# Row maximum of attention scores: one matmul over high and low parts of 128 rows, or two of 64 rows on the two halves of the array

## The reference

```python
qkv = X @ W_qkv + b_qkv                      # (4, 1024, 16 heads x 3 x 64)
Q, K, V = split(qkv)
scores = einsum('bhqd,bhkd->bhqk', Q, K) / sqrt(64)
attn = softmax(scores, axis=-1)
out = einsum('bhqk,bhkv->bhqv', attn, V) @ W_fc + b_fc
```

## Time and profile before

| | |
|---|---|
| median of 3 runs | 1964.52 us (1964.1 to 1965.58) |
| span of the profiled execution | 1962.0 us |
| TensorE busy (matmul) | 1813.4 us, 92% |
| VectorE busy | 1567.3 us, 80% |
| GpSimd busy | 1166.7 us, 59% |
| ScalarE busy | 1081.5 us, 55% |
| mean granted TensorE clock | 0.977 |

### The profile page before, as it was taken

The page is one execution under the profiler, slowest core; times in us unless marked ns, Lnnn a source line. Parts: engine busy times, 40 slices in busy tenths (PEclk is TensorE's granted clock), DMA queues, the critical chain, the costliest instruction groups (busy, mean ns, idle before and its releaser), DMA issues. The chain is left out here.

```text
span 1962.0 us, 29122 instructions
## 1 busy us (share of the span) xinstructions
PE 1813.4 (92%) x7819; PEld 985.8 (50%) x7819; DVE 1567.3 (80%) x2879; ACT 1081.5 (55%) x2008; POOL 1166.7 (59%) x521
## 2 busy tenths in 40 slices
PE   4899999999999999999999999999999999956996
PEld 3444444445544445544444444445544444425886
DVE  5788888888788888888787878887788888677788
ACT  4455555555555555555555555555555555424874
POOL 4465666666666666666666666666666666722124
PEclk8899999999999999999999999999999999967999
DMA  2111111111111111111111111111111110100010
GB/s 88 45 37 33 38 35 35 33 37 37 37 37 37 27 37 28 36 37 37 37 37 32 37 32 34 35 37 37 37 37 37 27 37 28 50 22 22 23 38 27
DMA packets 51521, 70.64 MB, mean 36 GB/s; under 512 B 6269, under 2 KB 29338, under 8 KB 51482
## 3 DMA queue, kind: packets, MB, share of 16 engines
q1 hardware_dynamic: 51328, 70.15, 12.9%
q10 hardware_dynamic: 154, 0.03, 0.0%
HBM read 14.58 MB, written 2.10 MB: 8 GB/s over the span
## 5 line engine op out<-in xcount | busy, mean ns | idle before, releaser
L553 POOL TENSOR_TENSOR ACC<-ACC,PR 128x1024 f32<-128x1024 f32 x382 | 924.4, 2420 | 217.8 <-ACT PR L615 211.4
L615 ACT ACTIVATE PR<-ps_s 128x512 f32<-128x512 f32 x1024 | 555.8, 595 | 653.4 <-PE ps_s L819 648.7
L648 DVE TENSOR_REDUCE NMH<-ps_mx 128x1 f32<-128x512 f32 x1016 | 679.1, 677 | 290.4 <-PE ps_mx L805 286.5
L828 PE MATMUL ps_o<-PR,V 128*64 128x512 f32 x2048 | 548.9, 614 | 0.0
L805 PE MATMUL ps_mx<-KA,QA 128*128 128x512 f32 x1016 | 460.1, 454 | 57.4 <-DVE NMH L648 57.1
L805 PEld LDWEIGHTS ps_mx<-KA,QA 128*128 128x128 f32 x1016 | 190.9, 188 | 468.4 <-issue 243.6
L818 PE MATMUL ps_s<-QA,KA 128*128 128x512 f32 x1024 | 406.5, 397 | 0.0
L819 PE MATMUL ps_s<-QB,KB 128*128 128x512 f32 x1024 | 403.7, 394 | 0.0
L553 POOL TENSOR_TENSOR ACC<-PR 128x1024 f32<-128x1024 f32 x64 | 159.7, 2495 | 372.6 <-ACT PR L615 372.6
L683 DVE RECIPROCAL SUM<-SUM 128x128 f32<-128x128 f32 x256 | 241.0, 943 | 6.9 <-ACT SUM L592 5.0
L819 PEld LDWEIGHTS ps_s<-QB,KB 128*128 128x128 f32 x1024 | 192.7, 188 | 46.0
(11 more groups left out here) (188 smaller groups left out, 1627.2 us busy)
## 6 DMA issues: line engine op xcount, KB each, us to landing
hcur<-hT SPq DMA_DIRECT2D x32, 512.0 KB, 2.9
KA<-KA SPq DMA_DIRECT2D x128, 128.0 KB, 2.3
QB<-QA SPq DMA_DIRECT2D x128, 128.0 KB, 2.3
Wraw<-in_L_attn_W_qkv SPq DMA_DIRECT2D x32, 192.0 KB, 2.4
x<-in_L_attn_X SPq DMA_DIRECT2D x4, 512.0 KB, 5.3
Wfc<-in_L_attn_W_fc SPq DMA_DIRECT2D x32, 64.0 KB, 1.8
hT<-in_L_attn_X SPq DMA_DIRECT2D x4, 512.0 KB, 5.8
out<-e_res SPq DMA_DIRECT2D x7, 256.0 KB, 2.3
```

The costliest lines, as they stand in the source:

```text
L553: G.tensor_tensor(ACC[:, ch, :, :], a, PR[:, t, :, :], ALU.add).then_inc(added, 1)
L615: A.activation(PR[:, t, h, :], ps_s[:, h, :], ACT.Exp, scale=SCALE).then_inc(exp_done, 1)
L648: D.tensor_reduce(NMH[:, ch, h, i, kc:kc + 1], banks[:, kc, :], AX, ALU.max, negate=True).then_inc(mx_red, 1)
L828: last = T.matmul(ps_o[half(h), ch, :], V[:, u, t, half(h)], PR[:, t, h, :], start=(t == 0), stop=(t == 7))
```

## The change

`max_half` becomes `max_both_heads`. A group is no longer (head h, query block i) with both key halves, but (query block i, key half kc) with both heads. For each head the product takes only the partitions `half(h)` of `QA` and `KA`, 64 rows that hold the high parts: head 0 on the upper, head 1 on the lower half of the array's rows, into banks 0 and 1 of `ps_mx`. Both stand behind the scores, ahead of the unit and of P·V, and only the second one signals. VectorE reduces both banks with one instruction (128x2 from 128x1024). `mx_red` and `mx_done` count groups, so the pair waits until both banks are reduced. The low part of Q no longer enters the maximum, but it still enters the scores. The second copy of K high isn't read here any more, and the wait on `kdup` moves to the first scores of a pair. There are as many maximum matmuls and columns as before.

```diff
-        NMH = sb("NMH", [P, 2, 2, 4, 2])
+        NMH = sb("NMH", [P, 2, 4, 2, 2])
@@ place(s)
-                return 0, 1, i // 4, i % 4
+                return 0, 1, i // 2, i % 2
@@ VectorE
-            def reduce_max(m, ch, h, i, count, banks=ps_mx):
-                if h == 0 and i == 0:
+            def reduce_max(m, ch, i, kc, count, banks=ps_mx):
+                if i == 0 and kc == 0:
                     wait(dve, mx_both, 2 * m + ch - 1)
-                for kc in range(2):
-                    dve.wait_ge(mx_done, 2 * count - 1 + kc)
-                    D.tensor_reduce(NMH[:, ch, h, i, kc:kc + 1], banks[:, kc, :], AX, ALU.max, negate=True).then_inc(mx_red, 1)
-                if h == 1 and i == 3:
-                    dve.wait_ge(mx_red, 2 * count)
+                dve.wait_ge(mx_done, count)
+                D.tensor_reduce(NMH[:, ch, i, kc, :], banks[:, :, :], AX, ALU.max, negate=True).then_inc(mx_red, 1)
+                if i == 3 and kc == 1:
+                    dve.wait_ge(mx_red, count)
                     wait(dve, rows_t, 2 * m + ch - 1)
-                    D.tensor_tensor(NM[:, ch, :, :], NMH[:, ch, :, :, 0], NMH[:, ch, :, :, 1], ALU.min).then_inc(mx_both, 1)
+                    D.tensor_tensor(NM[:, ch, :, :].rearrange("p h i -> p i h"), NMH[:, ch, :, 0, :], NMH[:, ch, :, 1, :],
+                                    ALU.min).then_inc(mx_both, 1)
@@ TensorE
-            def max_half(m, u, ch, h, i, kc, count, banks=ps_mx, ahead=0):
-                if h == 0 and i == 0 and kc == 0:
+            def max_both_heads(m, u, ch, i, kc, count, banks=ps_mx, ahead=0):
+                if i == 0 and kc == 0:
                     pe.wait_ge(q_lo, 2 * m + ch + 1)
                     if ch == 0:
                         pe.wait_ge(k_hi, 2 * m + 2)
-                        pe.wait_ge(kdup[u], 64 * (m // 2 + 1))
-                wait(pe, mx_red, 2 * (count - ahead) - 1 + kc)
+                wait(pe, mx_red, count - ahead)
                 q = ch * 512 + i * P
-                T.matmul(banks[:, kc, :], QA[:, u, h, q:q + P], KA[:, u, h, kc * 512:(kc + 1) * 512],
-                         start=True, stop=True).then_inc(mx_done, 1)
+                for h in range(2):
+                    last = T.matmul(banks[:, h, :], QA[half(h), u, h, q:q + P], KA[half(h), u, h, kc * 512:(kc + 1) * 512],
+                                    start=True, stop=True)
+                last.then_inc(mx_done, 1)
@@ scores
+                    if ch == 0:
+                        pe.wait_ge(kdup[u], 64 * (n // 2 + 1))
@@ pair
                     scores(n, u, s)
                     if has(n + d):
-                        max_half(*grp, 0, 16 * n + s + 10)
+                        max_both_heads(*grp, 16 * n + s + 10)
...
-                    if has(n + d):
-                        max_half(*grp, 1, 16 * n + s + 10)
```

More of the change, by code:

```diff
@@ L398, in place @@
                 i = s + 2
-                return 0, 1, i // 4, i % 4
+                return 0, 1, i // 2, i % 2
             if s < 14:
                 i = s - 6
-                return 1, 0, i // 4, i % 4
+                return 1, 0, i // 2, i % 2
             i = s - 14
-            return 1, 1, i // 4, i % 4
+            return 1, 1, i // 2, i % 2
         UNITS = {0: ("k", 1, 0), 1: ("k", 1, 1), 2: ("sums", -1, 1), 3: ("q", 1, 0),
@@ L694, in first @@
                 for i in range(8):
-                    reduce_max(0, 0, i // 4, i % 4, i + 1, (ps_mx, ps_s)[i % 2])
+                    reduce_max(0, 0, i // 2, i % 2, i + 1, (ps_mx, ps_s)[i % 2])
                 dve.wait_ge(s_mask, 3)
@@ L699, in first @@
                 for i in range(2):
-                    reduce_max(0, 1, i // 4, i % 4, i + 9)
+                    reduce_max(0, 1, i // 2, i % 2, i + 9)
                 split_w(1, 1)
@@ L704, in pair @@
                 for s in range(16):
-                    d, ch, h, i = place(s)
+                    d, ch, i, kc = place(s)
                     if has(n + d):
-                        reduce_max(n + d, ch, h, i, 16 * n + s + 11)
+                        reduce_max(n + d, ch, i, kc, 16 * n + s + 11)
                     x = unit_at(n, s)
@@ L836, in first @@
                         for i in range(8):
-                            for kc in range(2):
-                                max_half(0, 0, 0, i // 4, i % 4, kc, i, (ps_mx, ps_s)[i % 2], 1)
+                            max_both_heads(0, 0, 0, i // 2, i % 2, i, (ps_mx, ps_s)[i % 2], 1)
                         pe.wait_ge(mx_both, 1)
@@ L842, in first @@
                 for i in range(2):
-                    for kc in range(2):
-                        max_half(0, 0, 1, i // 4, i % 4, kc, i + 8)
+                    max_both_heads(0, 0, 1, i // 2, i % 2, i + 8)
                 freed("q", 0, 1)
@@ L856, in pair @@
                 for s in range(16):
-                    d, ch, h, i = place(s)
-                    grp = (n + d, u if d == 0 else 1 - u, ch, h, i)
+                    d, ch, i, kc = place(s)
+                    grp = (n + d, u if d == 0 else 1 - u, ch, i, kc)
                     scores(n, u, s)
                     if has(n + d):
-                        max_half(*grp, 0, 16 * n + s + 10)
+                        max_both_heads(*grp, 16 * n + s + 10)
                     x = unit_at(n, s)
```

## The result

The changed kernel takes 2059.07 us (median of 4 runs, 2055.99 to 2065.22), the kernel before beside it 1965.05. The ratio is 1.0479, with a 95% interval of 1.0453 to 1.0504: slower, and above the forecast range of 1905 to 2040. The direction was forecast, the size was not: +94 us for +35.

What follows compares the result with a forecast made beforehand. The bound was taken as TensorE's order and spacing of work in 16 steps plus one VectorE wait per pair. 0.56 + 0.43 + 0.15 = +1.14 us a pair, +35 us over 31 pairs, gave 2000 us; range 1905 to 2040.

Steps and rivals of the forecast that it cites:

- Concurrent halves: In every step, the two 64-row maximum matmuls run together, taking about 0.22 us.
- drain: On TensorE, changing to or from row halves drains the array as column divisions do, 0.085 us.
- late load: On TensorE, weights after a change of division can't be loaded ahead, 0.105 us each time.
- (a): Rival: row halves need no drain and their weights load ahead; -1.7 us a pair, 1912 us; chance 0.20.
- (c): Rival: the two halves don't run together, 0.43 for 0.22; 4.5 us a pair, 2104 us; chance 0.08.
- TensorE term: TensorE's 16 steps: eight with k, q, v or fc +0.13 each, eight others -0.06; +0.56 us a pair.
- The other estimate of the prediction: Maximum pair's run by the Trainium skill's row-tile speedup: about 0.28 us, making the sum 1 us a pair higher.
- Step 15: TensorE waits there for VectorE's whole double reduction, idling 2.15 us instead of 1.64; +0.43 us a pair.
- Other waits: Steps 3 to 8: VectorE's two-input operations may meet GpSimd additions at other moments; 0.15 us a pair.
- (d): Rival: the longer TensorE idle in step 15 lowers its clock; 2040 us or more; chance 0.03.
- Rival (b): VectorE's earlier start puts the O x 1/sum product before GpSimd's addition; step 15's idle vanishes, 1930 us; chance 0.04.

Runs made afterwards that it cites:

- e6: The changed kernel with the O x 1/sum product reading O from PSUM (ScalarE's copy gone) and the minimum over key halves as a one-input reduction: 1940.6 us.
- e5: The kernel before with the O x 1/sum product reading O from PSUM and the minimum over key halves as a one-input reduction: 1910.0 us.
- e1: The changed kernel with the O x 1/sum product reading O from PSUM, ScalarE's copy of O gone: 1970.7 us, ratio 1.0009.
- e9: The changed kernel with one edit, the minimum over the two key halves taken by a reduction with one SBUF input: 1941.3 us, ratio 0.9867.
- e8: The kernel before with an unread 32-column reciprocal on VectorE behind the O x 1/sum product of step 13: 1991.2 us, ratio 1.0128.
- e7: As e6, but in steps with k, q, v or fc the maximum pair stands behind the unit, just ahead of P·V: 1894.4 us, ratio 0.9630.
- e4: The changed kernel with its order and one reduction, but each maximum matmul takes all 128 rows again: 2036.7 us, ratio 1.0341.

## Why the prediction was right or wrong

- **Concurrent halves, drain, late load: right.** 0.51 busy for a pair of 504 ns; drains in and out; L761's load not done ahead. Rivals (a) and (c) are out.
- **TensorE term, 0.56 a pair: mis-sized, 1.05 measured** (e6 less e5). The run of the pair was taken as 0.22, though the prediction's own rows put one undivided matmul at 0.235. The pair with its drain takes the 0.32 of one 128-row matmul, and the drain into the halves is 0.09 for 0.085: some 0.02 more in each of 16 steps. Behind a return to 128 rows the unit's own matmuls are some 0.02 later besides. The k and q steps got +0.17 to +0.19, v and fc +0.13 to +0.17, plain, sums and rows steps -0.03 to -0.05, where I had +0.13 and -0.06. The other estimate of the prediction, 0.28 for the pair, would make it 0.47 from the pair to the next start; it is 0.42 to 0.43 in e6. A figure counted 24 times a pair must be right to a few ns.
- **Step 15, +0.43: right within 0.1.** Counted as in the forecast, the idle is 2.11 for 2.15 (1227.63 + 0.32 to 1230.06; 2.04 in the record); the pair without a fall is 1.50 longer, less 1.05 and less 0.1 of step 7 (3.74 for 3.64 in e6) leaves 0.35. L651 and L687 held by GpSimd as read from the rows; e1 and e9 show it by undoing it.
- **Other waits, 0.15: 0.10.**
- **The step that failed: "(d) The longer idle lowers TensorE's clock", put at 0.03.** The sum kept the clock at 1.00 and treated 0.5 us more idle as 0.5 us more time, on the argument that 1.49 us had left the clock at 1.00. That row showed only that the kernel stood on the safe side, not how far. It costs 1.71 us a pair, 53 us, more than everything else, and it is the whole of what lies outside the range: at 53.46 us a pair the time would have been about 1965 + 47 = 2012 us.
- **Rival (b)** did not happen by itself, and for the reason given. Brought about in e9 it gives 1941 us.

## What to carry to other kernels

Where TensorE has one regular idle of some length, look at what a slightly longer one would do to the granted clock, and give that case a real chance. Here 0.20 us more idle in the kernel before (e8) cost 0.73 us a pair, and taking 2.04 us of idle from the changed kernel (e9) gave back 3.92. Put a matmul on part of the array beside another that already divides it, so that the array goes back to 128 rows once and not twice (1.57 us a pair in e7). An elementwise operation of VectorE with two SBUF inputs, however small, can be held for a whole GpSimd operation; with one input in PSUM or as a reduction it was not.

## What the runs showed of the hardware

The same idle length gives a fall of the clock in some pairs and not in others: 12 falls at 1.69 us, 21 at 1.89, 30 at 2.04, none at 1.49, in some 31 pairs. No run here shows what picks the pairs. A fall costs 1.65 us in e8 and 1.84 in the changed kernel, where 4 of 26 last twice as long. Every run but the kernel before also has one or two falls between 140 and 165 us, in pair 1, at or just behind a single idle of 1.68 to 2.72 us; the counts include them. The kernel before has an idle of 2.05 us there and no fall.

The kernel before may itself be close to falling: its 13 runs beside e1 to e4 go from 1965.0 us at a mean granted clock of 0.977 to 1973.1 at 0.970. No trace of the longer ones was kept.

Two 64-row matmuls on the two row halves start within the same 0.01 us and together take what one 128-row matmul takes. A change into the halves drains 0.085 to 0.095 us, and the return from them to 128 rows costs 0.196 (e7 less e6), its load in the open of 0.105 included.
